# Causal mask of the shifted scores: one full-width product per bank, or four 32-column tiles and three more contraction rows

## The chip, the cores and the metric

One core of one Trainium2 chip. The time is the device time of one execution in microseconds (us), median of three runs. A core has five engines with a program each: PE (TensorE, matmuls), DVE (VectorE), ACT (ScalarE), POOL (GpSimd) and SP (SyncE, which here only issues DMAs). They meet at semaphores.

## What is computed

An adaLN block on x of 4 x 512 x 256: layer norm, modulation, a transformer block (attention with 32 heads of 8, then a gated MLP), a gated residual, a second norm and modulation, and a feed-forward part with eight low-rank experts of which two are picked. The change touches the attention alone:

```python
q = _apply_rope(q, cos, sin)
k = _apply_rope(k, cos, sin)
attn = jnp.einsum('bhqd,bhkd->bhqk', q, k) * scale
blk = math.ceil(S / num_blocks)              # 512 / 4 = 128
block_ids = pos // blk
block_mask = block_ids[:, None] != block_ids[None, :]
causal_mask = pos[:, None] < pos[None, :]
attn = jnp.where(causal_mask | block_mask, mask_floor, attn)
attn = jax.nn.softmax(attn, axis=-1)
context = jnp.einsum('bhqk,bhkd->bhqd', attn, v)
```

So each block of 128 queries sees only the 128 keys of the same block, and of these only those at or before the query.

## The kernel before

The four rows of the batch are worked one after another: a loop `Fori(0, B - 1)` over three rows, and the last row written out behind it. Ahead of the loop stands a preamble (loading and splitting the weights, the first row's norm, its projections of q, k and v, and its rope). Inside a row the attention comes first, then the output projection, the MLP, the second norm and the feed-forward part. The next row's norm and projections are mixed into the row that runs, which is why the code has `row + ahead`.

Activations lie with features on the partitions. For fp32-like accuracy operands are split into a high and a low part. For the scores of 4 heads at a time, `stack_tile` (L379) lays q and k out by DMA in `q_st` and `k_st`: three bands of 32 partitions (high and low parts), `PARTS * 32 = 96` rows. Rows 96 to 99 (`MROW` to `KS`) hold minus the row maximum of the four heads in `q_st`, and 1.0 in `k_st`, where a memset in the preamble has set rows 96 to 127 to 1.0.

Attention of a row is 8 units (`UNITS`): 4 blocks of 128 queries times 2 halves of 16 heads. A unit n/2 has two slots, a = 0 and 1, each of 8 heads in two PSUM banks. For a unit:

- `scores_for_max` (L1362): two mask products (`masked`, L1358, one to a bank) and two score products on 32 rows each (L1376) give scores, queries on the partitions. DVE takes their maximum (`unit_max`, L1000). It runs two units ahead of the rest.
- `max_transposed` (L1382): PE transposes the negated maximum (L1386), ACT puts it into rows 96 to 99 of `q_st` (`max_to_rows`, L719).
- `spread_queries` (L515): POOL writes `q_ex`, which has q once for each of the 4 heads, times 0 or 1 from the table `head` (L527 and L530).
- `shifted_scores` (L1389): two mask products (L1359), then two products of `k_st` (100 rows, 128 keys) with `q_ex` (100 rows, 4 x 128 queries) (L1402). This gives score minus maximum, keys on the partitions. ACT takes the exponential of both banks (L735).
- `contexts` (L1406): value and denominator products (L1424), each of 128 columns into one of four column tiles of 32.

The mask products add -1e30 where a key is not allowed: the weights are a 128 x 128 identity (`mask[:, 0, :]`), the moving operand is the mask of the block (`mask[:, 1, :]` or its transpose `mask[:, 2, :]`) repeated for four heads, 512 columns of bf16. They open the accumulation in the bank and the score product closes it.

The order on each engine is the order of the code. In a row PE runs, for each unit, slot 0 of `shifted_scores`, slot 0 of `scores_for_max` of the unit two later, the same for slot 1, then both `contexts`, then `max_transposed` (L1433 to L1441). Units 6 and 7 have no `scores_for_max` and no `max_transposed` left. The three pairs of banks are handed out by the table `fills` (L337).

In the preamble SP's queue issues, in order: loads of x, the constants, weights (L404 to L424), the mask (L410), then `stack(0, 0)` (L468, 3 x 12 DMAs by L391), then `highs_back` for the four tiles (L470, 4 x 4 DMAs by L442). POOL's `spread_keys` (L510) waits for the second four of these, PE's first `scores_for_max` waits for it. POOL issues the fourth 12 of the stack. DVE in the preamble runs `head_columns`, `centre`, `inverse`, `chunk_lows` of three chunks, `front_columns`, `front_modulation`, `front_scale` and so on (L1235 to L1249).

## Time and profile before

| what | value |
|---|---|
| median of 3 runs | 754.25 us (749.91, 754.25, 754.58) |
| profiled execution, its own time | 749.13 us |
| its span, first to last instruction | 747.3 us |
| mean granted TensorE clock | 0.943 |
| PE busy | 649.1 us, 87% |
| DVE, ACT, POOL busy | 410.6, 321.7, 224.9 us |

How to read the profile: one execution is recorded. A group of instructions is named by its line, engine and operation and by what it writes and reads; x is the count. "PE" is the matmul, "PEld" the weight load ahead of it, "SPq" SP's DMA queue.
### The profile page before, as it was taken

To read this page: it belongs to the slowest core of one execution; us is meant where nothing else is said; L and a number is where in the kernel's file an instruction comes from. 1 tells how busy PE (TensorE), PEld (TensorE's weight loads), DVE (VectorE), ACT (ScalarE), POOL (GpSimd) and SP (SyncE) were. 2 spreads that over 40 slices of the span, in tenths; PEclk is the share of its full clock that TensorE was granted. 3 is DMA by queue.
4 is the path that set the end of the run, shared out by engine and by line. 5 is a ranking of instruction groups with operands and counts; after the bars stand their busy time and mean duration, and the time that the engine had idled before them with its cause. 6 is when DMAs were issued, how large, how long until landed. Compare 5 with 4: busy or idle time off the path is not lost.

```text
span 747.3 us, 12089 instructions
## 1 busy us (share of the span) xinstructions
PE 649.1 (87%) x4536; PEld 441.6 (59%) x4536; DVE 410.6 (55%) x617; ACT 321.7 (43%) x472; POOL 224.9 (30%) x292
## 2 busy tenths in 40 slices
PE   3770799899999899999999899999999899868996
PEld 2750355667785466657785466657785466637673
DVE  1553456367746564368646564368646564436544
ACT  3332245636544246526534246525533444414442
POOL 3023576204201476115001476115001674010000
PEclk9995799999999899999998799999999899977998
DMA  8245120002302100003202110003202100000000
GB/s 334 71 144 144 33 59 1 2 0 72 99 1 56 61 28 2 1 0 98 72 1 57 51 36 2 1 1 96 73 1 56 57 2 2 1 0 1 0 1 28
DMA packets 16466, 32.62 MB, mean 44 GB/s; under 512 B 5280, under 2 KB 5920, under 8 KB 16160
## 3 DMA queue, kind: packets, MB, share of 16 engines
q1 hardware_dynamic: 14880, 28.74, 12.8%
q0 software_dynamic: 1536, 3.15, 1.5%
q8 instruction: 40, 0.66, 0.4%
q14 instruction: 10, 0.08, 0.0%
HBM read 12.99 MB, written 2.10 MB: 20 GB/s over the span
## 4 chain that ended last, share of the span: by engine, by line
PE 64%; issue 13%; DVE 8%; ACT 7%; SPq 4%; POOL 2%; DMA 1%; DVEq 0%; POOLq 0%; ACTq 0%
PE bank L1424 7%; PE bank L1359 7%; PE bank L1259 7%; PE bank L1260 6%; PE bank L1261 6%; PE bank L1376 3%; PE bank L1402 3%; SPq L391 3%; PE bank L1565 3%; PE bank L1567 3%; PE bank L1566 2%; PE bank L1386 2%; PE bank L1456 2%; ACT tile_f L735 2%; ACT arena L636 2%
## 5 line engine op out<-in xcount | busy, mean ns | idle before, releaser
L1000 DVE TENSOR_REDUCE arena<-bank 128x8 f32<-128x1024 f32 x64 | 77.9, 1223 | 80.8 <-PE bank L1376 80.6
L1359 PE MATMUL bank<-mask 128*128 128x512 bf16 x256 | 83.5, 410 | 29.5 <-POOL k_wide L510 26.2
L1191 DVE TENSOR_TENSOR arena<-arena,bank 128x512 f32<-128x512 f32 (+1 forms) x72 | 49.1, 687 | 82.1 <-ACT arena L785 81.6
L1259 PE MATMUL bank<-n_hi,w_lo 128*128 128x512 f32 x200 | 86.4, 432 | 8.4 <-DVE n_lo L1055 6.0
L785 ACT ACTIVATE arena<-bank 128x512 f32<-128x512 f32 (+1 forms) x72 | 42.5, 596 | 102.1 <-PE bank L1567 53.5
L1260 PE MATMUL bank<-n_lo,w_hi 128*128 128x512 f32 x200 | 80.3, 401 | 0.0
L1261 PE MATMUL bank<-n_hi,w_hi 128*128 128x512 f32 x200 | 80.1, 401 | 0.0
L510 POOL TENSOR_TENSOR k_wide<-n_lo,head_of 128x512 fp32r<-128x512 f32 x32 | 33.1, 1039 | 153.1 <-PE bank L1567 139.4
L735 ACT ACTIVATE tile_f<-bank 128x1024 f32<-128x1024 f32 x64 | 64.2, 1023 | 33.5 <-PE bank L1402 33.4
L719 ACT CAST q_st<-bank 4x512 fp32r<-4x512 f32 x32 | 18.5, 579 | 115.4 <-PE bank L1386 115.4
L530 POOL TENSOR_SCALAR arena_r<-q_st,const 100x512 fp32r<-100x512 f32 x96 | 64.9, 693 | 0.2
L1424 PE MATMUL bank<-tile_f,v_ex 128*32 128x128 f32 x1024 | 52.9, 275 | 2.5 <-ACT tile_f L735 2.5
L1402 PE MATMUL bank<-arena_r,k_st 100*128 100x512 f32 x128 | 54.5, 508 | 0.0
L1176 DVE TENSOR_TENSOR arena_r<-arena,arena_r 128x512 fp32r<-128x512 f32 (+1 forms) x72 | 52.0, 725 | 4.0 <-ACT arena_r L801 3.2
L1359 PEld LDWEIGHTS bank<-mask 128*128 128x128 bf16 x256 | 18.1, 103 | 59.5 <-issue 52.9
L1424 PE MATMUL bank<-tile_f,ones_ex 128*32 128x128 f32 x1024 | 52.3, 273 | 0.0
L1259 PEld LDWEIGHTS bank<-n_hi,w_lo 128*128 128x128 f32 x200 | 38.5, 193 | 22.8 <-DVE n_lo L1055 10.5
L1021 DVE RECIPROCAL arena<-bank 128x128 f32<-128x128 f32 x32 | 30.6, 957 | 37.0 <-PE bank L1424 37.0
L527 POOL TENSOR_TENSOR arena_r<-q_st,const 100x512 fp32r<-100x512 f32 x32 | 33.3, 1041 | 53.4 <-ACT q_st L719 53.4
L801 ACT CAST arena_r<-arena 128x512 fp32r<-128x512 f32 (+1 forms) x72 | 44.1, 613 | 7.5 <-PE bank L1261 4.8
L1260 PEld LDWEIGHTS bank<-n_lo,w_hi 128*128 128x128 f32 x200 | 38.6, 193 | 9.6 <-issue 1.9
L1261 PEld LDWEIGHTS bank<-n_hi,w_hi 128*128 128x128 f32 x200 | 38.4, 192 | 9.5
(158 smaller groups left out, 1263.0 us busy)
## 6 DMA issues: line engine op xcount, KB each, us to landing
q_st<-arena_r SPq DMA_DIRECT2D x96, 64.0 KB, 2.0
k_st<-arena_r SPq DMA_DIRECT2D x48, 64.0 KB, 2.5
k_st<-arena_r POOLq DMA_DIRECT2D x48, 64.0 KB, 2.5
h_next<-in_x SPq DMA_DIRECT2D x4, 512.0 KB, 3.3
tile_f<-in_x SPq DMA_DIRECT2D x4, 512.0 KB, 4.3
out<-arena SPq DMA_DIRECT2D x4, 512.0 KB, 2.6
arena<-in_wmod SPq DMA_DIRECT2D x1, 1536.0 KB, 10.1
n_hi<-q_st SPq DMA_DIRECT2D x24, 64.0 KB, 2.0
```

Source lines behind the costliest of these rows:

```text
L530: last = nc.gpsimd.tensor_scalar(q_ex[u % 2][0:KS, :, hh, :], src, con("head")[0:KS, hh:hh + 1], 1.0, ALU.mult, ALU.mult)
L735: nc.scalar.activation(prob[a], slot(("s2", n)).rearrange("p a s -> p (a s)"), ACT.Exp, scale=SCALE).then_inc(exp_done.sem, 1)
L801: nc.scalar.copy(ff_hl[j % 4][0][0:width], pair_tmp[j % 2][0:width]).then_inc(ff_hi.sem, 1)
L1000: nc.vector.tensor_reduce(neg_max[:, 2 * a:2 * a + 2, MROW:KS], slot(("s1", n)).rearrange("p a (h s) -> p a h s", s=P), AX_X, ALU.max, neg ...
L1176: nc.vector.tensor_tensor(to, pair_tmp[j % 2][0:width], ff_hl[j % 4][0][0:width].bitcast(F32), ALU.subtract)\
L1191: nc.vector.tensor_tensor(pair_tmp[n % 2][0:width], silu_out[n % 2][0:width], up, ALU.mult)\
L1259: nc.tensor.matmul(to, wl[rows, w_cols], ah[rows], start=start, stop=False)
L1260: nc.tensor.matmul(to, wh[rows, w_cols], al[rows], start=False, stop=False)
L1261: return nc.tensor.matmul(to, wh[rows, w_cols], ah[rows], start=False, stop=stop)
L1359: nc.tensor.matmul(to, mask[:, 0, :], mask[:, which:which + 1, :].broadcast_to([P, GH, P]), start=True, stop=False)
L1402: last = nc.tensor.matmul(to[:, g, :], k_st[0:KS, half * GQ + gq, blk * P:(blk + 1) * P], q_ex[u % 2][0:KS, gq], start=False, stop=True)
L1424: last = nc.tensor.matmul(tile, weights, prob[a][:, at:at + P], start=a == j == kind == 0, stop=a == j == 1, skip_group_check=True)
```

## The change

The mask of the shifted scores is built in another way. Let the 128 keys and 128 queries of a block be four tiles of 32. Only in the four tiles on the diagonal is the mask a triangle; in the others it is all or nothing. The triangles are written by four matmuls per bank (`masked_tiles`), each with 32 columns of the identity as weights and 4 x 32 columns of mask, into 32 partitions of PSUM, 128 matmul columns each. The tiles below the diagonal of the transposed mask come with the score product, which gets three more contraction rows (`KC` = 103 for `KS` = 100): row t (1 to 3) of `k_st` is 1 for keys from 32t on, and row t of `q_st` is -1e30 for queries before 32t. The mask products of `scores_for_max` stay.

The three rows are constant and are set once, in the preamble: DVE makes a table `below` from the mask, and six DMAs on SP's queue copy single partitions of it, repeated 32 times, into `q_st` and `k_st`; a seventh extends the table of heads (`head_rows`) by three rows of ones. PE and POOL each get one wait for these seven, ahead of the loop.

```diff
+TILE = P // 4
+KC = KS + P // TILE - 1
...
+            sp.wait_ge(ones_set.sem, 1)
+            sp.wait_ge(below_known.sem, 3)
+            sp.dma_start(head_rows[KS:KC, :], k_st[KC:2 * KC - KS, 0, 0:GH].bitcast(F32)).then_inc(coarse_set.sem, 16)
+            for t in range(1, P // TILE):
+                for n, dest in enumerate((q_st, k_st)):
+                    sp.dma_start(dest[KS + t - 1:KS + t].rearrange("p g (b c) -> p (g b) c", c=P).bitcast(F32),
+                                 below[t * TILE:t * TILE + 1, n, :].unsqueeze(1)
+                                 .broadcast_to([1, HEADS // GH * BLOCKS, P])).then_inc(coarse_set.sem, 16)
             sp.wait_ge(v_proj.sem, v_proj.count(0, 2))
...
-                src = q_st[0:KS, half * GQ:(half + 1) * GQ, blk * P:(blk + 1) * P].bitcast(F32)
...
+                src = q_st[0:KC, half * GQ:(half + 1) * GQ, blk * P:(blk + 1) * P].bitcast(F32)
...
                 for hh in range(1, GH):
-                    last = nc.gpsimd.tensor_scalar(q_ex[u % 2][0:KS, :, hh, :], src,
-                                                   con("head")[0:KS, hh:hh + 1], 1.0, ALU.mult, ALU.mult)
+                    last = nc.gpsimd.tensor_scalar(q_ex[u % 2][0:KC, :, hh, :], src,
+                                                   head_rows[0:KC, hh:hh + 1], 1.0, ALU.mult, ALU.mult)
...
             pool.wait_ge(heads_known.sem, 2)
+            pool.wait_ge(coarse_set.sem, (2 * (P // TILE) - 1) * 16)
...
+            def masked_below():
+
+                dve.wait_ge(mask_loaded.sem, 16)
+                nc.vector.tensor_copy(head_rows[:], con("head")).then_inc(below_known.sem, 1)
+                nc.vector.tensor_copy(below[:, 0, :], mask[:, 2, :]).then_inc(below_known.sem, 1)
+                nc.vector.tensor_scalar(below[:, 1, :], mask[:, 2, :], 0.0, None, ALU.is_ge).then_inc(below_known.sem, 1)
...
             chunk_lows(range(EARLY_CHUNKS))
+            masked_below()
             front_columns()
...
+            def masked_tiles(to):
+
+                for r in range(0, P, TILE):
+                    rows = slice(r, r + TILE)
+                    nc.tensor.matmul(to[rows].rearrange("p (h s) -> p h s", s=P)[:, :, rows], mask[:, 0, rows],
+                                     mask[:, 2:3, rows].broadcast_to([P, GH, TILE]), start=True, stop=False,
+                                     skip_group_check=True)
...
                     for g in range(2):
-                        masked(to[:, g, :], 2)
+                        masked_tiles(to[:, g, :])
                     for g in range(2):
                         gq = 2 * a + g
-                        last = nc.tensor.matmul(to[:, g, :], k_st[0:KS, half * GQ + gq, blk * P:(blk + 1) * P],
-                                                q_ex[u % 2][0:KS, gq], start=False, stop=True)
+                        last = nc.tensor.matmul(to[:, g, :], k_st[0:KC, half * GQ + gq, blk * P:(blk + 1) * P],
+                                                q_ex[u % 2][0:KC, gq], start=False, stop=True, skip_group_check=True)
...
             pe.wait_ge(ones_set.sem, 4)
+            pe.wait_ge(coarse_set.sem, (2 * (P // TILE) - 1) * 16)
```

PE's program in a unit, before, from the transposes of the maximum to the first rows of the contexts (L1359 is the mask product, L1402 the shifted score product, L1376 the score product for the maximum):

```order
L1386 MATMUL bank<-const,arena 100x128 x4
L377 ISA
L1355 REGISTER_ALU
L1359 MATMUL bank<-mask 128x512 x2
L1402 MATMUL bank<-arena_r,k_st 128x512 x2
L1366 REGISTER_ALU
L1359 MATMUL bank<-mask 128x512 x2
L1376 MATMUL bank<-k_wide,n_hi 128x512 x2
L1359 MATMUL bank<-mask 128x512 x2
L1402 MATMUL bank<-arena_r,k_st 128x512 x2
L1359 MATMUL bank<-mask 128x512 x2
L1376 MATMUL bank<-k_wide,n_hi 128x512 x2
```

The same place after the change (L1390 is in `masked_tiles`, L1383 in `masked`, L1434 the shifted score product, L1408 that for the maximum):

```order
L1418 MATMUL bank<-const,arena 100x128 x4
L383 ISA
L1379 REGISTER_ALU
L1390 MATMUL bank<-mask 32x4x32 x8
L1434 MATMUL bank<-arena_r,k_st 128x512 x2
L1398 REGISTER_ALU
L1383 MATMUL bank<-mask 128x512 x2
L1408 MATMUL bank<-k_wide,n_hi 128x512 x2
L1390 MATMUL bank<-mask 32x4x32 x8
L1434 MATMUL bank<-arena_r,k_st 128x512 x2
L1383 MATMUL bank<-mask 128x512 x2
L1408 MATMUL bank<-k_wide,n_hi 128x512 x2
```

Two of the four mask pairs of a unit have become eight small matmuls each; nothing has moved past anything else.

SP's queue in the preamble, before, from the stack of the first row to the copies of its high parts:

```order
L391 DMA q_st<-arena_r 32x512 x12
L391 DMA k_st<-arena_r 32x512 x12
L391 DMA q_st<-arena_r 32x512 x12
L442 DMA n_hi<-arena_r 32x512 x4
L442 DMA n_lo<-arena_r 32x512 x4
```

And after the change:

```order
L397 DMA q_st<-arena_r 32x512 x12
L397 DMA k_st<-arena_r 32x512 x12
L397 DMA q_st<-arena_r 32x512 x12
L478 DMA head_rows<-k_st 3x4
L481 DMA q_st<-below 1x32x128
L481 DMA k_st<-below 1x32x128
L481 DMA q_st<-below 1x32x128
L481 DMA k_st<-below 1x32x128
L481 DMA q_st<-below 1x32x128
L481 DMA k_st<-below 1x32x128
```

The seven new DMAs stand between the stack and the sixteen copies, which follow them as before.

## Rows read from the trace of the kernel before

**Rows 1.** The page: busy time by engine; the chain that ended last.
```profile
PE 649.1 (87%) x4536; PEld 441.6 (59%) x4536; DVE 410.6 (55%) x617; ACT 321.7 (43%) x472; POOL 224.9 (30%) x292
...
PE 64%; issue 13%; DVE 8%; ACT 7%; SPq 4%; POOL 2%; DMA 1%; DVEq 0%; POOLq 0%; ACTq 0%
```
**Rows 2.** Windows: stretch, us, busy time (count) by engine, PEclk, DMA share, GB/s.
```profile
90.00:138.00 48.00, 46.24 (x667) 29.89 (x665) 26.91 (x33) 27.03 (x33) 31.64 (x42) 1.00 0.08 24
...
409.00:420.00 11.00, 9.19 (x23) 3.49 (x22) 7.65 (x8) 0.58 (x1) 3.19 (x5) 0.66 0.13 51
```
**Rows 3.** The chain that ended last, 257 to 272 us: start, us, what.
```profile
263.77 1.89 PE bank L1424 x64
...
269.90 1.89 PE bank L1424 x64
```
**Rows 4.** Timeline of one unit: start, us, engine, line, operation, count, idle before.
```profile
266.07 0.59 PE L1359 MATMUL bank<-mask 128*128 128x512 bf16 x2
...
266.98 0.61 PE L1359 MATMUL bank<-mask 128*128 128x512 bf16 x2
...
267.51 0.18 PEld L1376 LDWEIGHTS bank<-k_wide,n_hi 32*128 32x128 f32 x2 [0.42 <-issue]
...
267.94 0.61 PE L1359 MATMUL bank<-mask 128*128 128x512 bf16 x2
267.95 2.03 POOL L530 TENSOR_SCALAR arena_r<-q_st,const 100x512 fp32r<-100x512 f32 x3
...
268.17 0.41 PEld L1402 LDWEIGHTS bank<-arena_r,k_st 100*128 100x128 f32 x2
...
269.83 0.42 PE L1424 MATMUL bank<-tile_f,v_ex 128*32 128x128 f32 x8
...
270.07 0.40 PE L1424 MATMUL bank<-tile_f,ones_ex 128*32 128x128 f32 x8
...
271.38 0.40 PE L1424 MATMUL bank<-tile_f,ones_ex 128*32 128x128 f32 x8
...
271.71 0.40 PEld L1386 LDWEIGHTS bank<-const,arena 128*100 128x100 f32 x4 [0.20 <-issue]
```
**Rows 5.** The chain that ended last in unit 4 of the second row.
```profile
281.14 1.03 ACT tile_f L735
...
282.22 0.60 PE bank L1359 x2
```
**Rows 6.** Timeline of SP's queue, 40 to 82 us.
```profile
46.15 7.57 SPq L391 DMA_DIRECT2D q_st<-arena_r  x12
```
**Rows 7.** The chain that ended last, 34 to 84 us.
```profile
71.48 0.45 issue
...
76.08 1.04 POOL k_wide L510
...
77.36 1.01 PE bank L1359 x2
```
**Rows 8.** The tile `mask`: ns min/median/max, first and last start; its DMA's landing.
```profile
L1359 PE MATMUL bank<-mask x256: 376/379/650, 77.4 to 630.1; 128*128 128x512 bf16 x128
L410 SPq DMA_DIRECT2D mask<-in_masks x1: 463/463/463, 7.3 to 7.3; - x1
...
mask<-in_masks SPq DMA_DIRECT2D x1, 96.0 KB, 13.2
```
**Rows 9.** Timeline of the weight loads behind the last contexts, last row.
```profile
633.08 0.30 PEld L1456 LDWEIGHTS bank<-arena,w_plain 128*128 128x128 f32 x2 [0.20 <-issue]
633.62 0.19 PEld L1456 LDWEIGHTS bank<-arena,w_plain 128*128 128x128 f32 x1 [0.24 <-issue]
```
**Rows 10.** Timeline of DVE in the preamble, and L1023 in a unit.
```profile
18.22 6.29 DVE L906 TENSOR_TENSOR w_lo<-tile_f,w_hi 128x1600 fp32r<-128x1600 f32 x3 [1.24 <-ACT w_hi L631]
...
55.48 0.18 DVE L883 COPY mod_all<-bank 128x32 f32<-128x32 f32 x1
...
266.72 0.29 DVE L1023 TENSOR_TENSOR arena<-bank,arena 128x128 f32<-128x128 f32 x1
```

More of the change, by code:

```diff
@@ L183, in adaln_kernel @@
         head_of = sb("head_of", [P, GH])
+        head_rows = sb("head_rows", [P, GH])
+        below = sb("below", [P, 2, P])
         head_sums = sb("head_sums", [P, GQ, GH])
@@ L287, in adaln_kernel @@
         heads_known = signal("heads_known", 0)
+        below_known = signal("below_known", 0)
+        coarse_set = signal("coarse_set", 0)
         k_spread = signal("k_spread", UNITS)
@@ L524, in spread_queries @@
                 pool.wait_ge(max_rows.sem, max_rows.count(row, u + 1))
-                src = q_st[0:KS, half * GQ:(half + 1) * GQ, blk * P:(blk + 1) * P].bitcast(F32)
-                nc.gpsimd.tensor_tensor(q_ex[u % 2][0:KS, :, 0, :], src,
-                                        con("head")[0:KS, 0:1].unsqueeze(2).broadcast_to([KS, GQ, P]), ALU.mult)
+                src = q_st[0:KC, half * GQ:(half + 1) * GQ, blk * P:(blk + 1) * P].bitcast(F32)
+                nc.gpsimd.tensor_tensor(q_ex[u % 2][0:KC, :, 0, :], src,
+                                        head_rows[0:KC, 0:1].unsqueeze(2).broadcast_to([KC, GQ, P]), ALU.mult)
                 for hh in range(1, GH):
-                    last = nc.gpsimd.tensor_scalar(q_ex[u % 2][0:KS, :, hh, :], src,
-                                                   con("head")[0:KS, hh:hh + 1], 1.0, ALU.mult, ALU.mult)
+                    last = nc.gpsimd.tensor_scalar(q_ex[u % 2][0:KC, :, hh, :], src,
+                                                   head_rows[0:KC, hh:hh + 1], 1.0, ALU.mult, ALU.mult)
                 last.then_inc(q_spread.sem, 1)
```

## The prediction

> **What bounds the kernel now.** I read the page first: PE is busy 87% of the span, the next engine (DVE) 55%, and the chain that ended last is 64% PE [rows 1]. So time taken off PE is worth something only where PE is the engine waited for, and I went on by stage. The windows show four attention stages of about 50 us, one for each row of the batch; in the first PE is busy 46.2 of 48 us and the granted clock is 1.00 (2.4 GHz) [rows 2]. In them one unit of 128 queries and 16 heads takes 6.12 us: the first context product comes at 263.77 and at 269.90 in the chain [rows 3]. The timeline of one unit then shows PE without a gap that another engine makes: transposes, mask pair and score pair for a=0, the pair for the maximum, the same for a=1, contexts [rows 4]. POOL's spread of the queries ends at 269.98, 1.7 us before the transposes at 271.71 that come ahead of its use, so it isn't waited for. Not every unit is like that. In units 4 and 5 of the first three rows ScalarE also does the norm of the next row and loads a table, and the chain goes through it: the exponential at 281.14 ends, and only then the mask of L1359 at 282.22 starts [rows 5]; unit 5 shows the same pattern. PE time saved just ahead of those waits is lost. Last, the preamble: from 46 to 77 us PE has almost nothing to do and the chain is SP, which issues one DMA after another, 12 in 7.5 us [rows 6], until the copy that `k_wide` needs lands and the first score product can begin at 77.36 [rows 7].
>
> **Removed and added on PE.** A slot of `shifted_scores` had two mask products of 512 columns; it gets two groups of four of 128 columns, each on a column tile of 32. The trace of one unit shows the pieces:
> - One mask product takes 0.21 us: a pair lasts 0.59 (266.07) and one record 0.379 [rows 4, 8], so the starts are 0.21 apart. The two keep the array for 0.43, and the weights of L1402 load behind the second (at 268.17, when that starts). From the slot's first instruction at 267.94 to the first real score column is 0.44.
> - A group of four on column tiles: the context product is the nearest row. Six sets of eight of its matmuls lie between 270.07 and 271.38, 0.218 us each, so four share 0.109 us, and their starts are spread over 0.02 (0.40 − 0.27 − 0.109). Those are fp32 halves; at the bf16 rate of the mask, 0.21 us for 512 columns, a group of 128 columns should need 0.054. This I take. The weight load of the first group costs 0.02: the first eight take 0.24, 269.83 to 270.07, and not 0.22.
> - Leaving column tiles costs a stop. The last context matmul starts at 271.51 (271.38 + 0.40 − 0.27), has its 0.11 and would be through at 271.62; the next full-width weight load starts at 271.71 [rows 4]. That is 0.09 us in which neither stream nor weight load runs, and the load then comes in the open: of the two loads for L1456 at 633.08 the second starts at 633.19 (633.08 + 0.30 − 0.19), which is when the first product's stream begins, 0.11 after its load; the stream then holds the next load until 633.62 [rows 9]. It isn't the semaphore wait there: from the full-width mask to the 32-row tiles of L1376, which wait for nothing, the gap is the same (second mask starts at 267.21, through at 267.42, load at 267.51) [rows 4].
> - Entering from full width is not in the trace for columns without another wait; for rows it is the 0.09 just read, and I take that. Entering from the row tiles costs no more than before: 0.43 from 267.51 to 267.94 into full width, and the context tiles at 269.83 follow theirs alike.
>
> New slot: 0.02 load + 2 × 0.054 + 0.02 spread + 0.09 stop + 0.107 open load = 0.35 us against 0.44. So a=1, which comes from row tiles, gains 0.09 to 0.10. For a=0, which comes from the transposes, the stop on entering (0.09) eats it: a loss of 0.01. A unit gains 0.08 us of 6.12, although 0.64 us of array time went out of it. The last unit of each row is better: its first slot comes from the contexts, where full width now pays a stop (the 0.09 and 0.20 of 271.71 again) and column tiles don't: 0.10 + 0.09 = 0.19. Per row: units 0 to 3 give 4 × 0.083 = 0.33, units 4 and 5 nothing where ScalarE is waited for, the last two units 0.18, together 0.51; the last row has no such wait in units 4 and 5, so 0.67. Sum 3 × 0.51 + 0.67 = 2.2 us gained.
>
> The Trainium skill (TensorEngine Tiling (Array Packing), Key Properties) says that changing the tiling mode, and not just the tile, drains the engine. The rows above carry the same thing with its size. By the count of columns alone, without that rule, the change would be worth some 12 us, which is the first rival.
>
> **Added rows of the product.** L1402 contracts over 103 rows in place of 100, POOL's four operations of a unit cover 103 partitions. Both run by their free size; if anything followed the rows it would be 3% of the 2.03 us of L530 [rows 4], 0.06 us, under 1.7 us of slack. Nothing. Without that cover it would be 32 × 0.06 = 2 us.
>
> **Added in the preamble, DVE.** Three operations stand between the last early `w_lo` (18.22 + 6.29, about 24.5 [rows 10]) and the columns of the modulation. DVE waits for nothing there, and the norm, the projections and the stack all follow from it. The mask has landed by then (7.3 + 13.2 = 20.5 us) [rows 8]. A copy of 4 columns is like the one of 32, 0.18. The two on 128 × 128 are not shown: at least that, at most the two-input operation on 128 × 128 at L1023, 0.29 [rows 10]. I take 0.235 each: 0.65 us in all, everything behind is late by that; bounds 0.5 to 0.8.
>
> **Added in the preamble, SP.** Seven DMAs go in between the stack and the copies for L442. Their waits are met long before (`ones_set` early, `below_known` at 25 us). Each holds the queue: 12 took 7.57 us, 0.63 each, whatever the engine that moves the data [rows 6]. Behind them wait eight copies, and for the eighth POOL, and for POOL the first score product [rows 7]; nothing hides it. 7 × 0.63 = 4.4 us. The lower end is the issue of the mask's load, 0.463, and 0.04 between two: 7 × 0.5 = 3.5 [rows 8]; the upper end, with two gaps of 0.45 as ahead of the second four copies [rows 7], 5.3. POOL's and PE's new waits for the seven are met when they come, since the DMAs that those waited for already stand behind them in the queue.
>
> **Sum**, on the profiled execution (749.13 us, span 747.3): +4.4 + 0.65 − 2.2 = +2.8, so 752.0. The three timed runs have median 754.25 (two near 754.4, one at 749.91), 5 us above the profiled one; the same difference on the median is 757.0, and as one of three lies low I take 756.5. With the bounds: the preamble 4.0 to 6.1; on PE, if entering from full width costs nothing, 18 slots gain 0.09 more, 1.6, so 3.8 gained; and nothing gained if ScalarE's waits reach further than units 4 and 5. Together 0 to +6 us.
>
> **Rivals.**
> *Columns count, stops don't.* If the weights of L1402 load beside the tiles and no stop comes, a slot ends at 0.02 + 0.054 + 0.107 = 0.18, a gain of 0.26. With 44 slots where PE is waited for (3 × 8 + 12 in whole units, 8 in the tails) that is 11.6 us, less 5.05: −6.5, so 747 us. Against it: the gap of 0.09 in [rows 4], from columns and from rows, with and without a wait. 8%.
> *Tiles don't run four abreast at bf16 rate.* Then the time goes the other way. If a group needs what the fp32 groups need, 0.109, a slot costs 0.11 more: 44 × 0.11 = 4.8, so 756.5 + 4.8 = 761; if the four run one after another, 4 × 0.054 = 0.21 a group, it is 44 × 0.32 = 14 us, so 770. It turns slower than before, even without the preamble, from a group time of 0.08 us. For it: no row has a bf16 column tile, and its output is strided. Against it: the context groups spread by 0.02, far below 0.05. 12%.
> The Trainium skill (TensorE: Matmul & The Clock Gate, section "Wait — 56ns, not 53.3ns?") has a least start-to-start of about 25 ns for a matmul however short. Eight in a row would then need 0.20 us, which is this rival at its first price; the starts within a context group, 0.02 for four, speak against it for separate tiles.
> *The clock falls.* The array gets less to do; from 409 to 420 us, at the start of a row's attention and with waits in it, PE was busy 9.19 of 11 us and the granted clock was 0.66 [rows 2]: 7.5 us at the low level of 1.2 GHz, which cost at most 3.7. A low stretch a third as long in each row is +5, 761.5 us, over twice the 2.2 gained; a whole one is +15. The point is a fall that takes more than 2.2 us in all. Against it: the stage has 1.00 over 48 us with PE's own stops already in it. 10%.
> *The preamble's issues are hidden.* Then −4.4 from the forecast, 752.1 us. The chain of [rows 7] has no room for it. 5%.
>
> **How the numbers follow.** Forecast with its own bounds 65%. Range 750 to 763: the forecast's bounds with the spread of the runs shown (749.9 to 754.6), the hidden preamble, and the lighter halves of the second and third rival; outside lie the first rival and 770. A measurement tells about 1% (7.5 us) from no change: faster than 746.7 needs the first rival, whose 747 lies at that border, or a mishap of the sum, 6%; slower than 761.8 needs the heavier part of the second or third rival (10%) or the forecast's upper end in a slow run (6%), 16%; the rest, 78%, is within 1%.
>
> **What would show it.** In a slot of the new profile: eight records of 128×32 tiles with two groups 0.05 to 0.06 apart; the weight load of the score product 0.14 to 0.15 after the last of them starts, and 0.35 from the slot's first instruction to the first score column; 0.2 from the last transpose to the first tile load. A unit at 6.0 to 6.05 us. The first `k_wide` near 81 us and not 76. If groups start 0.1 or more apart, or the weight load comes right behind the last tile, or the granted clock in 90 to 138 us is below 0.97, my account is wrong.

## The result, and the profile after the change

| | median | runs | ratio to before |
|---|---|---|---|
| before, same job | 752.69 us | 4 (749.91 to 754.58) | |
| changed kernel | 768.51 us | 4 (761.28 to 769.12) | 1.0217, 95% interval 1.0148 to 1.0287 |

The change makes the kernel slower, by 2.2% (1.5 to 2.9%); 756.5 us was forecast, in a range that ended at 763. In the table of the experiments the ratios leave out runs more than 1.5% above the fastest of the same kernel, which medians and means keep, so the ratio of `e8_before_filled` is that of its three fastest runs of ten and that of `e6_stops` of two of four. The profiled execution took 768.93 us, span 767.1 against 747.3: 19.8 us more. The page of the changed kernel, as in [rows 1], and its row of the granted clock in 40 slices:

```profile
PE 661.3 (86%) x4920; PEld 442.9 (58%) x4920; DVE 409.6 (53%) x620; ACT 321.4 (42%) x472; POOL 224.9 (29%) x292
...
PEclk9995579999999689999999589999999799976998
```

The same row of the kernel before, from its page:

```profile
PEclk9995799999999899999998799999999899977998
```

The two differ around the starts of the four attention stages, where the new row is lower by up to two tenths (one digit is a tenth higher), and by a tenth once behind the last one. PE is busy 12 us longer, although 0.6 us of streaming per unit was taken out of it. First the parts that the forecast worked out, in the timeline of one unit of the changed kernel. L1390 is the tile products, L1434 the score product, L1383 the full-width masks left in `scores_for_max`, L1418 the transposes, L1456 the contexts; it answers to [rows 4].

```profile
284.21 0.18 PEld L1408 LDWEIGHTS bank<-k_wide,n_hi 32*128 32x128 f32 x2 [0.42 <-issue]
...
284.64 0.30 PE L1390 MATMUL bank<-mask 128*32 128x128 bf16 x8
...
284.87 0.30 PEld L1434 LDWEIGHTS bank<-arena_r,k_st 103*128 103x128 f32 x2
284.87 0.72 PE L1434 MATMUL bank<-arena_r,k_st 103*128 103x512 f32 x2
...
285.43 0.12 PEld L1383 LDWEIGHTS bank<-mask 128*128 128x128 bf16 x2 [0.27 <-issue]
```

A slot of eight tile products lasts from 284.64 to the first weight load of the score product at 284.87, 0.23 us. The second load starts at 284.98 (284.87 + 0.30 − 0.19), where the first column of scores goes in: 0.34 us after the slot's start, where 0.35 was forecast and 0.44 stood before. The eight records of about 0.22 fit in 0.30, so two groups are 0.055 apart and the four of a group 0.01. The time to the next full-width mask is 0.79 us (284.64 to 285.43), against 0.92 before (267.94 to the next mask at 268.86).

Entering from the transposes costs the stop that was assumed. The first row stands for the transposes, the second for the tiles behind them:

```profile
282.30 0.64 PE L1418 MATMUL bank<-const,arena 128*100 128x128 f32 x4
...
282.87 0.12 PEld L1390 LDWEIGHTS bank<-mask 128*32 128x32 bf16 x8 [0.18 <-issue]
```

Four transposes last 0.64 with 0.27 for the last, which starts at 282.67; the load comes 0.20 later. In the last row of the batch PE is the only thing waited for up to the last two units, and there the chain that ended last shows the unit's length:

```profile
612.20 1.88 PE bank L1456 x64
618.18 1.88 PE bank L1456 x64
624.18 1.88 PE bank L1456 x64
```

That is 5.99 us in place of 6.12, a gain of 0.13 where 0.08 was forecast. The preamble, SP's queue, answers to [rows 6]:

```profile
62.94 7.52 SPq L397 DMA_DIRECT2D q_st<-arena_r  x12
70.58 0.76 SPq L478 DMA_DIRECT2D head_rows<-k_st  x1
71.39 0.53 SPq L481 DMA_DIRECT2D q_st<-below  x1
71.96 0.59 SPq L481 DMA_DIRECT2D k_st<-below  x1
72.59 0.59 SPq L481 DMA_DIRECT2D q_st<-below  x1
73.63 0.52 SPq L481 DMA_DIRECT2D k_st<-below  x1
74.20 0.58 SPq L481 DMA_DIRECT2D q_st<-below  x1
74.83 0.58 SPq L481 DMA_DIRECT2D k_st<-below  x1
75.52 2.43 SPq L448 DMA_DIRECT2D n_hi<-arena_r  x4
```

Seven issues hold the queue from 70.58 to 75.52, 4.9 us (4.4 forecast; there is one gap of 0.45, between 73.18 and 73.63, and the bounds of the forecast had room for two). The old gap of 0.45 ahead of the second four copies (71.48 in [rows 7]) is gone, so the queue's net share is 4.5. DVE's three operations, beside [rows 10]:

```profile
24.82 0.16 DVE L888 COPY head_rows<-const 128x4 f32<-128x4 f32 x1
24.89 0.22 DVE L889 CAST below<-mask 128x128 f32<-128x128 bf16 x1
25.03 0.22 DVE L890 TENSOR_SCALAR below<-mask 128x128 f32<-128x128 bf16 x1
25.16 0.16 DVE L896 COPY mod_all<-bank 128x16 f32<-128x16 f32 x1
```

They overlap: 0.34 us from 24.82 to 25.16 for what was priced at 0.65. The first score product starts at 83.33, 6.0 us later than the 77.36 of [rows 7]; of these, SP explains 4.5 and DVE 0.34. The rest, 1.2, doesn't belong to the change: the load of the constants that the chain begins with took 7.26 for 6.87 us, 0.39 more, and two stretches of projections on PE, at the same code, took 5.46 and 1.23 us for 5.04 and 0.87, which is 0.78 more, because there the clock rose later. The traces of `e2_full_mask` and `e3_tiles_four`, which have the same preamble, start at 82.70 and 82.29: 5.3 and 4.9 us later.

What was not priced is the rest. Stage by stage, between the same instructions of the two traces (first mask product, then the first output projection of each row, L1456 before and L1488 after):

| stretch | before | after | difference |
|---|---|---|---|
| start to first score product | 77.36 | 83.33 | +5.97 |
| attention of row 1 | 60.71 | 65.46 | +4.75 |
| to the end of attention, row 2 | 165.89 | 171.59 | +5.70 |
| row 3 | 168.35 | 170.70 | +2.35 |
| row 4 | 160.84 | 161.50 | +0.66 |
| rest | 114.15 | 114.52 | +0.37 |

The attention was to gain and it lost. The windows of the changed kernel say why (columns as in [rows 2]): 22 us from the first score product, and 26 us from the first mask product of the attention of rows 2, 3 and 4.

```profile
83.33:105.33 22.00, 19.28 (x124) 8.85 (x128) 7.97 (x9) 4.14 (x5) 9.63 (x13) 0.51 0.18 50
254.13:280.13 26.00, 23.68 (x153) 10.75 (x152) 13.47 (x15) 6.23 (x8) 11.01 (x15) 0.65 0.18 63
424.87:450.87 26.00, 23.67 (x153) 10.78 (x152) 13.43 (x15) 6.28 (x8) 11.06 (x15) 0.66 0.17 62
595.59:621.59 26.00, 24.44 (x232) 12.01 (x232) 15.07 (x17) 8.65 (x11) 13.16 (x18) 0.80 0.12 42
```

The same four stretches of the kernel before:

```profile
77.36:99.36 22.00, 19.27 (x180) 9.70 (x184) 11.20 (x12) 6.77 (x8) 14.06 (x19) 0.82 0.23 64
241.48:267.48 26.00, 23.61 (x203) 11.80 (x202) 15.77 (x18) 7.66 (x10) 14.72 (x19) 0.87 0.17 63
408.05:434.05 26.00, 23.99 (x194) 11.96 (x194) 14.75 (x16) 6.76 (x8) 13.42 (x17) 0.77 0.18 62
575.68:601.68 26.00, 23.00 (x203) 11.99 (x202) 16.31 (x17) 8.91 (x11) 13.41 (x18) 0.87 0.12 42
```

PE is busy as long as before, but the granted clock is 0.51 for 0.82, 0.65 for 0.87, 0.66 for 0.77 and 0.80 for 0.87: more of the time at 1.2 GHz. Behind these stretches the attention runs at 1.00 as before:

```profile
105.00:148.00 43.00, 40.69 (x673) 25.31 (x670) 23.54 (x30) 24.90 (x30) 28.56 (x38) 1.00 0.04 11
```

**A measure for the clock.** Each run lists its mean granted clock c. With two levels, 1.00 and 0.50, the time at the low one is 2 × (1 − c) × span; it is called low time below. It varies from run to run of one kernel. Over 25 runs of the kernel before it lay between 71 and 100 us, mean 89, and a straight line through these runs gives 0.35 us of time per us of low time; two other sets, of 7 and 23 runs, give 0.41 and 0.37. In the first row's attention of the two profiled executions, 0.31 × 22 / 0.5 = 13.6 us more of low time cost 4.75 us and what was gained there, 0.4 to 0.5: 0.39 per us. I use 0.39, and differences of a few us at an equal clock move with that choice by about 1; where PE waits for others, a slow clock costs nothing, so it isn't 0.5. Means of four runs scatter: the standard error of their low time is 2 to 6 us. The changed kernel has a mean low time of 119 us, 30 more.

### The profile page after: what moved, and what is told of

It is laid out like the page before. It is cut to its first block, busy times and chain, and to the rows that moved or that the text cites. A ratio compares the mean times of both kernels' runs of the same rounds, so it can differ in the third digit from the quotient of the medians.

```text
span 767.1 us, 12869 instructions
## 1 busy us (share of the span) xinstructions
PE 661.3 (86%) x4920; PEld 442.9 (58%) x4920; DVE 409.6 (53%) x620; ACT 321.4 (42%) x472; POOL 224.9 (29%) x292
## 4 chain that ended last, share of the span: by engine, by line
PE 60%; issue 13%; DVE 8%; ACT 7%; SPq 7%; DMA 2%; POOL 2%; DVEq 0%; POOLq 0%; ACTq 0%
PE bank L1456 8%; PE bank L1283 6%; SPq L397 5%; PE bank L1284 5%; PE bank L1285 5%; PE bank L1383 4%; PE bank L1434 4%; PE bank L1408 3%; PE bank L1597 3%; PE bank L1418 3%; PE bank L1599 2%; PE bank L1598 2%; ACT tile_f L751 2%; PE bank L1488 2%; PE bank L1652 2%
## 5 line engine op out<-in xcount | busy, mean ns | idle before, releaser
L1023 DVE TENSOR_REDUCE arena<-bank 128x8 f32<-128x1024 f32 x64 | 78.0, 1223 | 89.8 <-PE bank L1408 89.8
L1383 PE MATMUL bank<-mask 128*128 128x512 bf16 x128 | 46.2, 448 | 34.8 <-POOL k_wide L525 30.6
L545 POOL TENSOR_SCALAR arena_r<-q_st,head_rows 103x512 fp32r<-103x512 f32 x96 | 65.0, 694 | 0.2
L1456 PE MATMUL bank<-tile_f,v_ex 128*32 128x128 f32 x1024 | 55.2, 286 | 3.4 <-ACT tile_f L751 3.4
L1456 PE MATMUL bank<-tile_f,ones_ex 128*32 128x128 f32 x1024 | 54.3, 282 | 0.0
L542 POOL TENSOR_TENSOR arena_r<-q_st,head_rows 103x512 fp32r<-103x512 f32 x32 | 33.3, 1041 | 59.2 <-ACT q_st L735 58.1
L1434 PE MATMUL bank<-arena_r,k_st 103*128 103x512 f32 x128 | 50.2, 475 | 0.0
L1597 PE MATMUL bank<-arena_r,w_lo 128*128 128x512 f32 (+1 forms) x96 | 39.0, 406 | 3.8 <-DVE arena L1214 3.8
```

Source lines behind the costliest of these rows:

```text
L545: last = nc.gpsimd.tensor_scalar(q_ex[u % 2][0:KC, :, hh, :], src, head_rows[0:KC, hh:hh + 1], 1.0, ALU.mult, ALU.mult)
L1023: nc.vector.tensor_reduce(neg_max[:, 2 * a:2 * a + 2, MROW:KS], slot(("s1", n)).rearrange("p a (h s) -> p a h s", s=P), AX_X, ALU.max, neg ...
L1383: nc.tensor.matmul(to, mask[:, 0, :], mask[:, which:which + 1, :].broadcast_to([P, GH, P]), start=True, stop=False)
L1434: last = nc.tensor.matmul(to[:, g, :], k_st[0:KC, half * GQ + gq, blk * P:(blk + 1) * P], q_ex[u % 2][0:KC, gq], start=False, stop=True, s ...
L1456: last = nc.tensor.matmul(tile, weights, prob[a][:, at:at + P], start=a == j == kind == 0, stop=a == j == 1, skip_group_check=True)
L1597: nc.tensor.matmul(to, wl[:, cols], ah, start=False, stop=False, skip_group_check=True)
```

## The experiments

Theory A: the slots now give the array less full-width work, and where an attention stage starts with the clock low or undecided, it stays low longer. A1 puts it down to the missing columns, A2 to the stops. Theory B: the later preamble alone moved the starts of the stages against the clock's rises and falls, and the tiles have no part. In the expectations, "full-clock part" is time less half of the low time.

| kernel | median us | ratio to before (95%) | mean us | mean low time | mean − 0.39 × low |
|---|---|---|---|---|---|
| before (25 runs) | 753.5 | | 752.4 | 89.3 | 717.6 |
| changed | 768.5 | 1.0217 (1.0148 to 1.0287) | 766.9 | 119.4 | 720.3 |
| e1_late | 761.8 | 1.0133 (1.0032 to 1.0234) | 761.4 | 117.0 | 715.8 |
| e2_full_mask | 759.6 | 1.0105 (1.0005 to 1.0206) | 759.4 | 98.1 | 721.1 |
| e3_tiles_four | 780.8 | 1.0414 (1.0311 to 1.0517) | 779.6 | 115.9 | 734.4 |
| e4_warm | 758.0 | 1.0104 (1.0005 to 1.0203) | 758.5 | 109.0 | 716.0 |
| e5_no_mask | 749.5 | 0.9943 (0.9908 to 0.9979) | 749.0 | 115.2 | 704.1 |
| e6_stops | 783.3 | 1.0320 (1.0209 to 1.0431) | 782.2 | 104.3 | 741.5 |
| e7_hoisted | 759.8 | 1.0101 (1.0052 to 1.0150) | 759.0 | 121.5 | 711.6 |
| e8_before_filled | 749.1 | 0.9872 (0.9807 to 0.9938) | 747.8 | 78.8 | 717.1 |
| e11_full_first_two | 755.5 | 1.0012 (0.9972 to 1.0052) | 754.6 | 94.9 | 717.6 |
| e12_tiles_first_two | 759.7 | 1.0091 (1.0051 to 1.0131) | 759.7 | 107.9 | 717.6 |
| e9_tiles_filled | 742.7 | 0.9853 (0.9779 to 0.9927) | 743.1 | 79.7 | 712.0 |
| e10_mixed_filled | 743.1 | 0.9876 (0.9819 to 0.9934) | 742.7 | 71.9 | 714.7 |

Of each profiled execution, the low time split at two points of every row: up to the first shifted score product (from the end of the row before, or from the start), from there to the end of the row's contexts ("in the units"), summed over the four rows, and what comes behind the last row's attention. It is taken from the clock records, which reach up to 2 us beyond the span:

| kernel | ahead of the units, us | in the units | behind |
|---|---|---|---|
| before | 49 | 10 | 27 |
| e8_before_filled | 58 | 0 | 30 |
| e2_full_mask | 68 | 10 | 25 |
| e11_full_first_two | 63 | 9 | 25 |
| changed | 71 | 28 | 27 |
| e1_late | 67 | 32 | 27 |
| e4_warm | 50 | 28 | 27 |
| e12_tiles_first_two | 67 | 25 | 24 |
| e7_hoisted | 45 | 40 | 31 |
| e5_no_mask | 59 | 43 | 27 |
| e6_stops | 51 | 31 | 28 |
| e3_tiles_four | 62 | 13 | 24 |
| e9_tiles_filled | 44 | 17 | 30 |
| e10_mixed_filled | 48 | 0 | 21 |

The middle column is the one in which the changed products run. With full masks alone, or with full masks in the first two units, it is 0 to 10 us; with one set of tiles there it is 25 to 40, and 17 with the fillers (e9). The column ahead of it varies from 44 to 71 and does not follow the masks: e2 has full masks and 68. So of the 41 us between the two executions before and after, 18 lie in the units and 23 ahead of them, of which 7 belong to the first row; that the tiles lengthen this part isn't shown.

**e1_late: the seven DMAs behind the copies that are waited for.**

```diff
+            sp.wait_ge(v_proj.sem, v_proj.count(0, 2))
+            for i in range(2):
+                sp.wait_ge(rope_hi.sem, rope_hi.count(0, i + 1))
+                highs_back(i, 0, 0)
             sp.wait_ge(ones_set.sem, 1)
             sp.wait_ge(below_known.sem, 3)
...
-            sp.wait_ge(v_proj.sem, v_proj.count(0, 2))
-            for i in range(4):
+            for i in range(2, 4):
                 sp.wait_ge(rope_hi.sem, rope_hi.count(0, i + 1))
                 highs_back(i, 0, 0)
...
-            pool.wait_ge(coarse_set.sem, (2 * (P // TILE) - 1) * 16)
             first_units(0, 0)
+            pool.wait_ge(coarse_set.sem, (2 * (P // TILE) - 1) * 16)
...
-            pe.wait_ge(coarse_set.sem, (2 * (P // TILE) - 1) * 16)
...
             pe.wait_ge(plain_loaded.sem, 9 * 16)
+            pe.wait_ge(coarse_set.sem, (2 * (P // TILE) - 1) * 16)
```

The seven DMAs stand between the two loops now, and POOL and PE wait for them only after the first units and the last loads of the preamble. e4 to e7 and e9 to e12 start from this kernel.

> The changed kernel with the seven DMAs of the coarse rows behind the first eight copies of SP's queue in place of ahead of them, and the waits of POOL and PE for them moved behind their first work. Theory A (the tiles give the array too little work where the clock is low, so the low stretches at the start of each attention stage get longer): the seven issues come off the chain, about -5 us, and the low stretches of 10 us at the starts of rows 2 and 3 stay: near 763 us. Theory B (the later preamble moved everything against the clock's steps, the tiles have no part): the low stretches go back to those of the kernel before, near 751. The old account, without any clock effect: 751.

761.8, as theory A has it (763). The preamble's part of the loss is real, 5.5 us on the means, and it is not the larger one: 117 us of low time stay, and against theory B's 751 the kernel is 10 us late. The last column, 715.8 against 717.6 before, is what the tiles gain at an equal clock: 1.8 us, or 2.1 with DVE's 0.34 taken out, where the forecast said 2.2. The agreement is closer than the measure: the four runs have a standard error of 1.1, and with 0.35 in place of 0.39 the gain would be 0.7.

**e2_full_mask: everything of the change but the tiles.**

```diff
-                        masked_tiles(to[:, g, :])
+                        masked(to[:, g, :], 2)
```

> The changed kernel with the full-width mask products put back into the shifted scores; the preamble, the 103 rows and all the rest of the change stay (the coarse rows then add -1e30 a second time where the mask already has it). Theory A: the low stretches at the starts of the rows are those of the kernel before (3 to 14 us per row), the time is before plus the preamble's 6 us: 759. Theory B: as long as in the changed kernel, about 20 us of low clock more in the preamble: 768 or more.

759.6 where A said 759. The low time is 98, of which 6 are the longer wait in the preamble, when PE has nothing to do: 92, like before. With the tiles and the same preamble it is 119, so B falls. Its four windows, as above:

```profile
82.70:104.70 22.00, 19.27 (x122) 8.90 (x122) 9.86 (x11) 5.88 (x8) 11.89 (x16) 0.67 0.20 58
250.18:276.18 26.00, 23.67 (x203) 11.91 (x202) 15.71 (x18) 7.67 (x10) 14.72 (x19) 0.86 0.17 63
417.18:443.18 26.00, 23.67 (x168) 11.45 (x170) 14.27 (x16) 6.76 (x8) 12.43 (x16) 0.72 0.17 62
586.50:612.50 26.00, 22.99 (x198) 11.60 (x198) 15.58 (x16) 8.04 (x9) 12.90 (x17) 0.83 0.11 41
```

In the first row it is 0.67 with full masks too: of the fall there from 0.82 to 0.51 only a part is the tiles'.

**e3_tiles_four: each set of tile products four times.**

```diff
-                    for g in range(2):
-                        masked_tiles(to[:, g, :])
+                    for again in range(4):
+                        for g in range(2):
+                            masked_tiles(to[:, g, :], again == 0)
```

> The changed kernel with each set of eight tile products issued four times (the repeats add -1e30 again where it already is), so that the tiles stream as long as the two full-width products did, 0.44 us a slot, and the two stops stay. At an equal clock it costs 6 x 0.055 = 0.33 us more in each of 44 slots, +14.5: 783. Theory A: the added work brings the clock back earlier, total low time falls from 128 us towards the 87 of the kernel before, up to -20: 763 to 773. Theory B: 783.

The size came out: the last column is 14.1 us above the changed kernel's, 14.5 forecast. The mean low time did not fall as A had it: 116, not 90 to 100. But its four runs had 99, 115, 124 and 127 us, and the one with 99 is the profiled one, with 0.69, 0.86, 0.67 and 0.87 in the four windows and 13 us in the units. So time on the array, spent in tiles of 32 columns between two stops, did not bring the clock back on the mean and nearly did in one execution; four runs do not settle how much it helps.

**e4_warm: filler in the preamble.** `e1_late` and, ahead of the first score product:

```diff
+            pe.wait_ge(high_back[0].sem, GQ * 16)
+            for _ in range(9):
+                nc.tensor.matmul(bank[:, 1, :], mask[:, 0, :], mask[:, 1:2, :].broadcast_to([P, GH, P]),
+                                 start=True, stop=True)
```

> Kernel e1_late with nine full-width mask products of 512 columns into an unused PSUM bank in the preamble, after the first four copies have landed and ahead of the first score product. Their results are never read. They should bring the granted clock to 1.00 before the first unit. Theory A and B alike: the first two units run at 2.4 GHz, which gives back half of the low stretch behind the first score product in e1_late (8 to 20 us long), so -4 to -10 us against e1_late. If the clock has no part in the loss: no change, or +1.

−2.9 us on the means and 8 us less of low time, short of the −4 to −10 that was expected; the intervals of e1 and e4 overlap, so four runs do not settle it alone.

**e5_no_mask: the columns gone, and no stop.** The triangles of the causal mask are left out of the shifted scores and the exponential's scale is divided by 64, so this computes something else.

```diff
-                    for g in range(2):
-                        masked_tiles(to[:, g, :])
...
-                                                q_ex[u % 2][0:KC, gq], start=False, stop=True, skip_group_check=True)
+                                                q_ex[u % 2][0:KC, gq], start=True, stop=True)
```

> Kernel e1_late without any mask product in the shifted scores: the score product opens the bank itself. The triangles on the diagonal are left out, the three coarse rows stay, and the exponential's scale is divided by 64 to keep the numbers finite, so the output is another one. So the column time is gone and no stop is added. At an equal clock a slot takes 0.33 us less than with full masks (0.43 less behind the transposes), 44 slots: 17 us under e2_full_mask. What is asked is the low time (twice the share below clock 1.00, times the span). If the missing columns keep the clock low (A1), it is as long as in e1_late (mean 117 us of four runs) or longer. If the stops of the tiles do (A2), it is that of e2_full_mask less the preamble's shift, near 90.

This tells A1 from A2. There is no stop that the kernel before didn't have, and the low time is 115, like e1's 117. Its windows at the first two starts, as above:

```profile
77.50:99.50 22.00, 19.27 (x114) 8.67 (x114) 9.49 (x11) 5.87 (x8) 11.10 (x15) 0.59 0.28 72
244.33:270.33 26.00, 23.81 (x145) 11.42 (x148) 14.06 (x16) 6.76 (x8) 11.27 (x15) 0.65 0.18 63
```

So missing full-width columns are enough to hold the clock down; with them PE also has less to do between its waits, and the scores have other values, which this run doesn't separate. At an equal clock, all of the mask in these slots is worth 13.5 us against the kernel before (17 was expected), and 10 of them go to the clock: 3 or 4 are left of it. The clock also fell again late in the stage, 36 to 43 us behind the first shifted score product, for 3 to 7 us in each of the first three rows, which neither the kernel before nor the changed one does.

**e6_stops: full masks and tiles.**

```diff
                     for g in range(2):
-                        masked_tiles(to[:, g, :])
+                        masked(to[:, g, :], 2)
+                    for g in range(2):
+                        masked_tiles(to[:, g, :], False)
```

> Kernel e1_late with the two full-width mask products AND the eight tile products behind them in each slot (the triangles are added twice). So all columns of the kernel before are there, and the stops on entering and leaving the tiles too. At an equal clock a slot takes 0.87 us in place of 0.44: +19 us on 44 slots against full masks, 722 us at full clock. Low time: A1 (missing columns) expects some 90 us as with full masks, time near 767; A2 (stops) expects 115 or more, time near 780.

A mean of 104 us, between the two answers, from four runs of 88 to 117, in a kernel that is 24 us longer than the kernel before at an equal clock (19 was expected). Its windows at the four starts:

```profile
78.59:100.59 22.00, 19.27 (x104) 8.07 (x108) 7.46 (x8) 4.13 (x5) 9.22 (x12) 0.50 0.17 36
253.88:279.88 26.00, 23.84 (x141) 10.98 (x140) 12.22 (x14) 4.71 (x6) 8.79 (x12) 0.61 0.18 63
430.76:456.76 26.00, 22.92 (x245) 11.10 (x244) 15.05 (x18) 7.81 (x10) 15.29 (x20) 1.00 0.18 63
600.12:626.12 26.00, 23.00 (x145) 10.26 (x144) 12.66 (x13) 6.52 (x8) 9.62 (x13) 0.69 0.12 41
```

In three rows of this execution the clock stays low in the units as long as with tiles alone (31 us in all, 28 in the changed kernel, 10 before), although no full-width column is missing; in the third row it was up at the start and stayed up. So this trace speaks for a part of the stops next to the columns. It is of one of the two longer runs, though; the two that the ratio rests on have 88 and 103 us, nearer to A1's 90. The question stays open.

**e7_hoisted: a unit's first tiles right behind the contexts, which run on column tiles already.**

```diff
-                    to = fill(row, "s2", n)
-                    for g in range(2):
-                        masked_tiles(to[:, g, :])
+                    to = fill(row, "s2", n) if a or not u else slot(("s2", n))
+                    if a or not u:
+                        for g in range(2):
+                            masked_tiles(to[:, g, :])
...
                         contexts(2 * u + a)
+                    if u + 1 < UNITS:
+                        ahead_of = fill(row, "s2", 2 * u + 2)
+                        for g in range(2):
+                            masked_tiles(ahead_of[:, g, :])
```

> Kernel e1_late with the tile products of a unit's first slot moved from behind the transposes to right behind the contexts of the unit before, which run on column tiles already. The stop between transposes and tiles (0.09) is gone in 7 units of each row, and one of leaving tiles is shared with the contexts' own: a slot behind the transposes becomes 0.11 (tiles) and a hidden load against 0.44, so a unit takes 5.8 us in place of 5.99. At equal clock 18 units x 0.19 to 0.2 = -3.5 us against e1_late, up to -6 with the tails. A1: low time as e1_late, 117. A2: with one stop of three gone, less, 100 to 110.

At an equal clock −4.2 us against e1, in the expected −3.5 to −6. The chain shows the unit: contexts start at 269.58 and 275.27, 5.69 us apart (5.8 expected), and the eight tiles behind them take 0.11.

```profile
269.58 1.88 PE bank L1460 x64
271.47 0.11 PE bank L1393 x8
271.58 0.57 PE bank L1421 x4
...
275.27 1.89 PE bank L1460 x64
```

One stop less did not shorten the low time (121, where A2 had 100 to 110), which speaks for A1, and nearly half of the time gained is lost: −2.4 us on the means.

**e8_before_filled: the kernel before, with filler.** The nine products of e4, and in each row:

```diff
                 for a in range(2):
                     scores_for_max(row, 2 + a, 0)
+                for _ in range(6):
+                    nc.tensor.matmul(bank[:, 1, :], mask[:, 0, :], mask[:, 1:2, :].broadcast_to([P, GH, P]),
+                                     start=True, stop=True)
                 max_transposed(1)
```

> The kernel before with full-width mask products into an unused PSUM bank as filler, their results never read: nine in the preamble ahead of the first score product, six in each row ahead of the wait for the maximum of unit 1 (2.3 us of waiting there). If the waits at the start of the attention stages are what lets the clock fall, the low time goes from 87 us (mean of seven runs) to 65 or less and the time falls by 8 to 12 us. If the fillers come at the wrong place, they cost up to 1 us per row and the low time stays: 754 to 757.

10 us less of low time (79, where 65 or less was expected) and, on the means, 4.5 us faster than the kernel before, 0.6%, where 8 to 12 us were expected. The sign is clear: work whose results nobody reads, put where PE waited for DVE anyway, makes the kernel faster.

**e11_full_first_two and e12_tiles_first_two: where it matters.** From `e1_late`; e12 has `u < 2` in place of `u >= 2`.

```diff
-                    for g in range(2):
-                        masked_tiles(to[:, g, :])
+                    if not (u >= 2):
+                        for g in range(2):
+                            masked(to[:, g, :], 2)
+                    elif True:
+                        for g in range(2):
+                            masked_tiles(to[:, g, :])
```

> Kernel e1_late with the full-width mask products in units 0 and 1 of each row and the tiles in units 2 to 7. Theory A1 with a place (the clock is low or undecided at the start of each attention stage, and the first units' missing full-width columns keep it there): low time falls from 117 us (e1_late) to that of the kernel before, 87 to 95, and the time is 703 to 704 at full clock + 46 = 750. If the columns are missed everywhere alike: a quarter of the way back, 110, time 759.

> The complement: tiles in units 0 and 1 of each row, full-width mask products in units 2 to 7. A1 with a place: low time 105 to 117 us, as with tiles everywhere, and the time is 707 + 56 = 763. Columns missed everywhere alike: 95, time 755.

Low time 95 with full masks in the first two of eight units, 108 with tiles in those two alone; 117 with tiles everywhere, 89 with none. If every unit counted alike, the first would be 110 and the second 96. The start of the stage carries most of it, about 19 to 22 of 28 us, and not all. The times, with medians of 755.5 and 759.7, lie between the two answers of each expectation (750 or 759, 763 or 755). The windows of e11 and of e12 from the first mask product of row 2:

```profile
247.55:273.55 26.00, 23.67 (x211) 11.78 (x210) 15.59 (x18) 7.87 (x10) 14.92 (x19) 0.87 0.17 63
```

```profile
246.75:272.75 26.00, 23.89 (x151) 10.86 (x150) 13.38 (x15) 5.94 (x8) 10.70 (x14) 0.64 0.18 63
```

0.87 is the kernel before, 0.64 the changed one. In the first row e11 doesn't differ from the kernel with tiles everywhere: 0.65, as in e1.

**e9_tiles_filled and e10_mixed_filled: both together.** e9 is e7 with the fillers of e8. e10 has in addition full masks in units 0, 1, 4 and 5 (0 and 1 in the last row).

> Kernel e7_hoisted (tiles in all units) with the fillers of e8_before_filled: nine full-width products in the preamble and six in each row at the wait for the maximum of unit 1. In e8 they took 10 us off the low time. If they do the same here: low time 121 - 10 = 111, full-clock part 698.5, time 754. If they are enough to bring the clock back for the thin units too: low time 80 and 740.

> Full-width mask products in units 0, 1, 4 and 5 (only 0 and 1 in the last row), tiles in the others with the first slot's hoisted behind the contexts, the late DMAs and the fillers. The full-clock part should be about half way between e8 (708.4) and e7 (698.3), 703; A1 with a place gives the low time of e8, 79, so 742 to 744, under both kernels and under e8 (747.8 mean). If tiles anywhere lengthen the low time: 115 and 760.

Both beat both kernels: e9 0.9853 of the kernel before (0.9779 to 0.9927) and so some 0.964 of the changed one (0.9853 / 1.0217). It is the better of the two answers: on the means of four runs low time went from 121 to 80, and not to 111. e9's windows at the preamble's filler and at row 2:

```profile
73.27:95.27 22.00, 20.01 (x157) 8.70 (x157) 8.67 (x11) 5.48 (x7) 11.62 (x15) 0.81 0.26 64
241.05:267.05 26.00, 24.14 (x287) 12.69 (x290) 17.02 (x20) 9.39 (x11) 17.30 (x23) 1.00 0.18 63
```

In rows 3 and 4 of the same execution, the one with the most low time of the four, it is 0.87 and 0.73, so the fillers do not hold the clock up at every start. The full masks of e10 on top gave 8 us less of low time (72, expected 79) and cost 2.7 at an equal clock; the time, 743.1, is in the expected 742 to 744, and the two kernels are not to be told apart.

## Why the prediction was wrong

Point by point:

- **The slot on PE: right.** 0.34 us against 0.35, groups 0.055 apart, the stop 0.09 on either side, load in the open. The rule of the Trainium skill (TensorEngine Tiling (Array Packing), Key Properties) that changing the tiling mode drains the engine agrees with these stops. The Trainium skill's least start-to-start of about 25 ns (TensorE: Matmul & The Clock Gate, section "Wait — 56ns, not 53.3ns?") does not hold between separate column tiles: four start within 0.01 us.
- **What a unit gains: right in kind, small in size.** 0.13 and not 0.08. From the tiles' start to the next mask it is 0.79 against 0.92 or 0.90; 0.03 to 0.04 of that lie in the score products, which the forecast left as they were. The sum held nevertheless, as far as the measures reach: 2.4 us by the traces and 2.1, uncertain by 1 or more, at an equal clock, against 2.2. That is partly luck, since too small a gain in a unit stood beside a gain at unit 7 that did not come. In the profiled executions the last row gained 0.9 (from the contexts of unit 0 to the output projection 40.38 for 41.26 us) and the others 0.12 or so in a unit ahead of those where ScalarE is waited for. The extra gain at the start of unit 7 did not show: there too ScalarE is waited for.
- **The preamble: right.** What belongs to the change is 4.5 us on SP's queue and 0.34 on DVE, 4.8 against 5.05; DVE's term was twice too large, and SP's issues, 4.9, a little too small. The other 1.2 of the 6.0 us are the slower load and the later clock of this execution.
- **More contraction rows: right.** POOL's operation takes 0.694 us on 103 partitions, 0.693 before.
- **The clock: the step that failed.** In the sum it stood at nothing, and as a rival it had 10%. Two things were wrong in it. The price that the range took in was that of one short stretch of about 2.5 us at 1.2 GHz per row, +5 us; the whole stretch, +15, was named and left outside. It is 30 us of low time in all on the means, of which 24 are not the preamble's wait; at 0.39 that is 9.4 us, the largest part of the loss. And the reason against it, that the stage holds 1.00 for 48 us, was taken from the part where the clock is up and stays up. In the changed kernel it stays up there too. What the rows of the kernel before did show was the start of the stage, 0.66 from 409 to 420 us, and that was the place to price.

Sum of the measured parts (the preamble's as in the profiled pair): 6.0 (preamble) + 9.4 (clock) − 2.4 (units, by the traces) = 13.0 us, against 14.5 on the means. Of e2 it gives 6.0 + 0.39 × 2.8 = 7.1 (measured 7.0), of e1 0.3 − 2.4 + 0.39 × 27.7 = 8.7 (9.0).

**What stays open.** That full masks in place of the tiles bring most of the low time back is shown (e2, e11), and that columns can do it without a stop is too (e5). How the loss of the changed kernel divides between columns and stops is not: the trace of e6 points to some part of the stops, its shorter runs and e7 to none. Nor is it known how much tile products as long on the array as the full masks (e3) help, since its runs reach from 99 to 127 us. And the low time ahead of the units, 44 to 71 us in one execution, has no cause shown.

## What to carry to other kernels

Read the granted clock at the starts of stages, after a wait, before taking streaming work off TensorE: where it is below 1.00 there, as 0.66 here, work removed can cost more than it saved, here 9 us through the clock for 2.4 us saved. Filler products of full width into an unused bank, placed in waits at such a start, gave back 10 us of low time alone and some 40 with the tiles; try them together with the saving. And a one-time setup of seven DMAs costs their issue in full, here 0.7 us each with the gaps, if it stands ahead of a transfer that something waits for.

## What the runs showed of the hardware that was not expected

- Four column tiles of bf16, 128 columns each, start within 0.01 us and take 0.055 us together; fp32 halves take 0.109.
- Leaving or entering column tiles is the same stop of 0.09 us, and next to the contexts, already on tiles, eight tile products take 0.11 us.
- The clock's mean over an execution of one unchanged kernel lay between 0.934 and 0.952, and the times of 746 and 755 us belong to it: 0.35 us per us of low time.
- Between full masks and no masks at all in half of the places, low time went from 89 to 115 us. Once up, the clock stayed up to the end of the stage in the kernel before and in the changed one (1.00); without the masks it fell again for 3 to 7 us in three rows, and with the hoisted tiles of e7 and e9 for 3 us in three rows, and in e11 in one.
- Three small DVE operations in a row cost 0.34 us, not the sum of their records, 0.60.
